# A new order of work around a second attention: who uses bank 0 in which unit, when weighted values run, one reduction for two blocks' maxima, and the split of the maxima on GpSimd

## The reference

```
q, k, v = (einsum('bld,dhe->blhe', x, W) for W in (Wq, Wk, Wv))     # 16 heads of 8
a = einsum('bqhd,bkhd->bhqk', q, k) / 8 ** 0.5
a = softmax(where(tril, a, -inf))
o = einsum('bhqk,bkhd->bqhd', a, v)
return einsum('blhe,hed->bld', o, Wout)
```

## Time and profile before

| what | value |
|---|---|
| median of three runs | 934.86 us |
| the profiled execution | 932.55 us, span 930.8 us |
| PE busy | 842.5 us (91%) |
| DVE busy | 728.3 us (78%) |
| ACT busy | 528.7 us (57%) |
| POOL busy | 465.4 us (50%) |
| mean granted clock of PE | 0.98 |
| the second attention | about 396 to 660 us |
| a middle sequence (1 to 4) of it | 33.24 us |

### The profile page before, as it was taken

How to read it: one execution, slowest core, us unless ns; L and a number is a source line. 1 busy time by engine, 2 the same in 40 slices (tenths; PEclk the granted TensorE clock), 3 DMA queues, 4 the chain that set the end, 5 groups by cost and what they waited for, 6 DMA issues and landing times. The chain is left out here.

```text
span 930.8 us, 17280 instructions
## 1 busy us (share of the span) xinstructions
PE 842.5 (91%) x5977; PEld 556.6 (60%) x5977; DVE 728.3 (78%) x1455; ACT 528.7 (57%) x771; POOL 465.4 (50%) x620
## 2 busy tenths in 40 slices
PE   5899999999778886689999999888889999999997
PEld 4677777775566655334444444443558767776875
DVE  6888998879899995888898998987666656565542
ACT  4677788789566675367777777767423223222311
POOL 4133222224568786236666666456464365345444
PEclk9999999999999999779999999999989999999999
DMA  9300000000000006765545446200000000000000
GB/s 284 93 12 12 11 11 11 0 13 0 16 1 12 1 12 130 142 129 117 111 82 126 106 85 127 52 4 14 12 1 24 1 23 23 23 0 23 11 12 12
DMA packets 36067, 43.79 MB, mean 47 GB/s; under 512 B 4878, under 2 KB 28094, under 8 KB 36000
## 3 DMA queue, kind: packets, MB, share of 16 engines
q1 hardware_dynamic: 36000, 42.93, 19.5%
HBM read 21.81 MB, written 15.09 MB: 40 GB/s over the span
## 5 line engine op out<-in xcount | busy, mean ns | idle before, releaser
L1877 ACT ACTIVATE PT<-PS 128x1024 f32<-128x1024 f32 x160 | 161.5, 1022 | 61.6 <-PE PS L1668 61.3
L1939 POOL TENSOR_SCALAR_AFFINE_SELECT PT<-PT 128x256 f32<-128x256 f32 (+1 forms) x224 | 97.3, 451 | 101.9 <-ACT PT L1877 99.9
L2368 POOL TENSOR_TENSOR PRE_sb<-PRE_sb,VA 128x512 f32<-128x512 f32 x64 | 82.3, 1285 | 125.8 <-DVE PRE_sb L2436 125.7
L2335 ACT ACTIVATE sg_d<-PS 128x512 f32<-128x512 f32 x64 | 38.1, 597 | 154.5 <-PE PS L1397 154.5
L2436 DVE TENSOR_TENSOR PRE_sb<-sg_d,PS 128x512 f32<-128x512 f32 x64 | 44.0, 688 | 79.6 <-ACT sg_d L2335 79.1
L465 ACT ACTIVATE E<-PS,m 128x512 f32<-128x512 f32 x128 | 85.7, 688 | 34.7 <-PE PS L351 25.8
L1979 DVE TENSOR_REDUCE negm<-PS 128x2 f32<-128x1024 f32 x64 | 77.8, 1221 | 20.0 <-PE PS L1657 19.6
L1684 PE MATMUL PS<-PT,VA 128*32 128x512 f32 (+3 forms) x1024 | 89.9, 446 | 3.6 <-POOL PT L1939 3.6
L1650 PE MATMUL PS<-kS,qS 52*128 52x384 bf16 (+3 forms) x512 | 64.3, 311 | 14.7 <-ACT PT L1877 6.9
L514 POOL TENSOR_SCALAR Qs<-Qs 128x1024 f32<-128x1024 f32 x32 | 34.5, 1080 | 81.6 <-ACT Qs L446 81.0
L1668 PE MATMUL PS<-qS,kS 55*128 55x384 bf16 (+3 forms) x512 | 63.4, 307 | 7.5 <-DVE negm L1979 3.5
(11 more groups left out here) (331 smaller groups left out, 2249.5 us busy)
## 6 DMA issues: line engine op xcount, KB each, us to landing
qk_rows<-parts SPq DMA_DIRECT2D x32, 192.0 KB, 2.8
qS<-qk_rows SPq DMA_DIRECT2D x32, 192.0 KB, 4.3
kS<-qk_rows SPq DMA_DIRECT2D x32, 192.0 KB, 4.6
xs_sb<-XN_sb SPq DMA_DIRECT2D x20, 256.0 KB, 2.3
qk_rows<-parts SPq DMA_DIRECT2D x32, 128.0 KB, 2.8
X_sb<-in_x_dram SPq DMA_DIRECT2D x8, 256.0 KB, 6.6
qk_rows<-parts SPq DMA_DIRECT2D x32, 64.0 KB, 2.5
out_dram<-X_sb SPq DMA_DIRECT2D x8, 256.0 KB, 2.3
```

Of the source, the lines that this page charges most:

```text
L1877: nc.scalar.activation(PT[:, quad % 2, u, :], PS[:, b:b + 2, :].rearrange("p b n -> p (b n)"), ACT.Exp).then_inc(exp_ready, 1)
L1939: nc.gpsimd.affine_select(out=v, in_=v, pattern=[[0, 4 if u == 4 else 2], [1, P]], compare_op=ALU.is_ge, fill=0.0, base=0, channel_multipl ...
L2368: nc.gpsimd.tensor_tensor(acts[:, s, f, :], acts[:, s, f, :], W[:, slot, s, :], ALU.mult).then_inc(weighted, 1)
```

## The change

Six things are changed in `attention1`. Bank 0 gets a new table of users: (0,2) OT, (0,4) maxima of half 1, (1,0) V, (1,2) on, (1,4) x, (2,0) q, (2,2) OT, (2,4) maxima of half 0 of the next sequence, (3,2) output, (3,4) k; what waits for what follows it, as do ACT's and DVE's copies. Weighted values of kt 0 run in u = 3; for quads 0 and 1 (and quad 3 of the last sequence) kt 1, 3 and 2 run as one batch in the next quad's u = 1. The two reductions of u = 2, 3 become one per 128 columns, with eight outputs; `negm` has three more slots, and `join_maxima` takes the smallest of the three partial negated maxima of block 2. The split's four instructions run on GpSimd within the periods (on DVE before the first). K's parts are made in (0,1) to (0,4) of the next period and not in quad 3 and (0,1); q's start in (2,1). `factor` moves from (1,0) to (1,1), and the residual `add` from (3,0) to (3,2).

```diff
+M_SLOT = (0, 2, 1, 3)
-        negm = sb("negm", [P, NT, 2, NPAIR])
+        negm = sb("negm", [P, NT + 3, 2, NPAIR])
-        MASK_SLOTS = [(2, 0), (2, 2), (3, 2), (3, 4)]
+        MASK_SLOTS = [(2, 0), (2, 4), (3, 0), (3, 4)]
+        def split_maxima(eng, engine, i, h):
+            ch = Steps(eng, max_steps, i * 2 + h, 4)
+            ch.n = 1
+            hs = slice(4 * h, 4 * h + 4)
+            nm, mr = negm[:, 3:7, :, hs], mrem[:, :, :, hs]
+            mp = lambda k: mpart[:, h, :, :, k, :]
+            ch.wait()
+            ch.link(engine.tensor_copy(mp(0), nm))
+            ch.link(engine.tensor_tensor(mr, nm, mp(0), ALU.subtract))
+            ch.link(engine.tensor_copy(mp(1), mr))
+            engine.tensor_tensor(mp(2), mr, mp(1), ALU.subtract).then_inc(m_parts, 1)
+            ch.end()
...
@@ tensor, weighted_v and period
-                pe.wait_ge(masked, (i * 4 + quad) * 7 + {0: 2, 1: 6, 3: 7}[kts[0]])
+                pe.wait_ge(masked, (i * 4 + quad) * 7 + {(0,): 2, (1,): 6}.get(kts, 7))
-                    if u == 4:
+                    if u == 3:
                         weighted_v(i, slot, quad, (0,))
+                        turn_ot(i - 1, 1)
+                    elif (quad, u) == (0, 4):
+                        if first:
+                            pe.wait_ge(m_row, 1)
+                        else:
+                            pe.wait_ge(o_normed, i * 2)
                         turn_maxima(i, 1)
-                    elif (quad, u) == (0, 3) and not first:
+                    elif (quad, u) == (1, 0) and not first:
                         pe.wait_ge(m_row, i * 2 + 2)
...
+                    elif (quad, u) == (2, 4):
+                        pe.wait_ge(o_normed, i * 2 + 1)
                         turn_maxima(i + 1, 0)
...
-                    elif (quad, u) == (3, 2) and ahead(i):
+                    elif (quad, u) == (3, 4) and ahead(i):
...
-                    if u == 0 or u == 1:
+                    if (quad, u) in ((1, 1), (2, 1)):
+                        weighted_v(i, slot, quad - 1, (1, 3, 2))
+                    elif u == 0 or u == 1:
...
-            weighted_v(LAST, LAST % 2, 3, (1,))
-            weighted_v(LAST, LAST % 2, 3, (3, 2))
+            weighted_v(LAST, LAST % 2, 3, (1, 3, 2))
@@ scalar, period
-                    elif (quad, u) == (0, 2):
+                    elif (quad, u) == (0, 4):
                         keep_maxima(i, 1)
...
@@ gpsimd, period
+                    if (quad, u) == (0, 0) and not first:
+                        split_maxima(pool, nc.gpsimd, i, 1)
+                    elif (quad, u) == (2, 0) and not last:
+                        split_maxima(pool, nc.gpsimd, i + 1, 0)
...
@@ vector, maxima, join_maxima, period
-                    nc.vector.tensor_reduce(negm[:, 2, :, pair], PS[:, b:b + 2, 0:384], AX.X, ALU.max, negate=True)
-                    ins = nc.vector.tensor_reduce(negm[:, 0, :, pair], PS[:, b:b + 2, 384:512], AX.X, ALU.max, negate=True)
+                    ins = nc.vector.tensor_reduce(negm[:, 0:4, :, pair].rearrange("p s r -> p r s"),
+                                                  PS[:, b:b + 2, :].rearrange("p b (s n) -> p b s n", n=P), AX.X, ALU.max, negate=True)
+            def join_maxima(i, h):
                 dve.wait_ge(max_read, i * 20 + 10 * h + 10)
                 hs = slice(4 * h, 4 * h + 4)
+                ins = nc.vector.tensor_reduce(negm[:, 3 + M_SLOT[2], :, hs], negm[:, 0:3, :, hs].rearrange("p s r a -> p r a s"), AX.X, ALU.min)
+                ins.then_inc(max_steps, 1)
...
-                    elif (quad, u) == (3, 0) and not first:
+                    elif (quad, u) == (3, 2) and not first:
                         add(i - 1)
```

More of the change, by code:

```diff
@@ L1731, in period @@
                         maxima(i + 1, 1 - slot, quad, u, ring(n))
-                    if u == 4:
+                    if u == 3:
                         weighted_v(i, slot, quad, (0,))
[L1735 to L1738, removed]
+                    if (quad, u) == (0, 2) and not first:
+                        if i <= LAST - 2:
                             pe.wait_ge(kf_ready, i + 3)
@@ L1778, in period @@
                         ex.turn_selection(pe, 0)
[L1779 to L1782, removed]
                     elif (quad, u) in MASK_SLOTS and last:
                         k = MASK_SLOTS.index((quad, u))
-                        pe.wait_ge(*(((ex.selT_ready, 1), (m_kept, 1), (att_added, i), (m_kept, 3))[k]))
+                        pe.wait_ge(*(((ex.selT_ready, 1), (o_normed, i * 2 + 1), (m_kept, 2), (att_added, i))[k]))
                         ex.mask(0, k).then_inc(m_ready, 1)
@@ L1788, in period @@
                         pr.project(pe, i + 3, 1 - slot, g.wq1, q_ready)
-                    elif (quad, u) == (2, 2) and not last:
+                    elif (quad, u) == (2, 2):
                         if ahead(i):
@@ L1814, in period @@
                         pr.project(pe, i + 3, 1 - slot, g.wk1, k_ready)
-                    if u == 0 or u == 1:
+                    if (quad, u) in ((1, 1), (2, 1)):
+                        weighted_v(i, slot, quad - 1, (1, 3, 2))
+                    elif u == 0 or u == 1:
                         kts = (1,) if u == 0 else (3, 2)
-                        if quad > 0:
-                            weighted_v(i, slot, quad - 1, kts)
-                        elif not first:
+                        if quad == 3:
+                            weighted_v(i, slot, 2, kts)
+                        elif quad == 0 and not first:
                             weighted_v(i - 1, 1 - slot, 3, kts)
@@ L1958, in period @@
                         (ex.low if part else ex.high)(pool, n)
-                    if (quad, u) == (1, 0) and first:
+                    if (quad, u) == (1, 1) and first:
                         factor_and_shift(nc, g, pool, 2 * LAST - 1, 2 * NB, 1, 2)
-                    elif (quad, u) == (1, 0) and i > 1:
+                    elif (quad, u) == (1, 1) and i > 1:
                         factor(i - 2)
                     elif (quad, u) == (0, 1) and behind(i):
+                        pr.first_part_on_pool(pool, i + 2, 1, kf_ready)
+                    elif (quad, u) == (0, 2) and behind(i):
+                        pr.first_rest(pool, i + 2, 1)
+                    elif (quad, u) == (0, 3) and behind(i):
+                        pr.second_part_on_pool(pool, i + 2, 1)
+                    elif (quad, u) == (0, 4) and behind(i):
                         pr.third_part(pool, i + 2, 1)
@@ L2105, in period @@
                         apply(i - 2)
-                    if opens(i, 1) and (quad, u) == (1, 0):
+                    if opens(i, 1) and (quad, u) == (1, 1):
                         ex.keep_x_low(dve, 0, 0)
@@ L2109, in period @@
                         ex.add_logits(dve, 0)
-                    elif opens(i, 1) and (quad, u) == (2, 4):
+                    elif opens(i, 1) and (quad, u) == (3, 0):
                         keep_first_u()
@@ L2123, in period @@
                         mask_first_high(0)
-                    elif last and (quad, u) == (2, 4):
+                    elif last and (quad, u) == (2, 3):
                         mask_first_low(0)
@@ L2133, in _ @@
                 if u == 4 and quad % 2:
-                    split_maxima(0, quad // 2)
+                    join_maxima(0, quad // 2)
+                    split_maxima(dve, nc.vector, 0, quad // 2)
             in_periods(dve, period)
```

113 lines of the change are left out of this document (48 added, 65 removed).

## The result

The changed kernel takes 926.06 us in the median (920.36 to 930.29) against 933.81 (928.85 to 937.58), 18 runs each: ratio 0.9914, 95% interval 0.9895 to 0.9932, 0.9% faster. The forecast was 922.9 (919.0 to 930.5), faster. The profiled execution took 926.10, its span 924.3, for 932.55 and 930.8: 6.5 us less, where the prediction's sum says 12.0.

The account below looks back on a forecast made before the run. PE was taken as the bound, stalling at short steps where maxima wait for the Exp before. Gains of 7.6, 1.2, 1.4, 1.2, 0.2 and 0.4 sum to 12.0 us: 932.55 to 920.55, plus 2.3 gives 922.9 (919.0 to 930.5).

Parts of the forecast that it names:

- Middle sequences: Four equal sequences of the second attention, each 1.9 us shorter (31.3 for 33.2): 7.6 us in all.
- the walk: Step-by-step timing of one sequence on the new table by start-to-start rules; remaining PE waits sum to 1.25 us.
- Sequence 5: Sequence without x, q, k for PE: 30.4 us for 31.6, a gain of 1.2.
- GpSimd's chain: The split's four small instructions on GpSimd, twice per sequence: 1.25 us, hidden with 0.7 to spare before kt 0.
- SP's: Maxima's copy two steps later, so SP issues k's parts and next rows 3 us later; claimed hidden.
- A: Rival: waits only moved; merges and half of DVE's relief leave 3 to 5 us, 931; chance 0.14.
- C: Rival: maxima's DMA as slow in every sequence as in the first, 38 us lost, 961; chance 0.02.
- D: Rival: eight outputs cost more, or PE's order isn't limited as read; within 0.2%, 935; chance 0.06.
- The first sequence: Quads 2 and 3 gain as in the middle, low clock in front: 1.2 us, plus 0.2 for the prologue.
- Sequence 6: Seventh sequence, counted from 0: 31.8 us for 33.2, a gain of 1.4.
- The last: Last sequence, no maxima, ACT leads: moved factor gives back 0.9, merge at the end costs 0.65; net 0.4 gained.
- the merged tail: End of the last sequence: merged kt 1, 3, 2 all wait for the last mask, 0.65 us more.

Follow-up runs that it names:

- the kernel with the selection first: Changed kernel, but in the last sequence's step (1,4) DVE copies the turned selection before the norm's apply; median 920.29 us, ratio 0.9891.
- the DVE half alone: Kernel before, old table, with only the joint reductions, the join and the split on GpSimd; median 934.37 us, ratio 1.0019.
- the kernel with the factor in halves: Changed kernel; last sequence: factor divided over (0,1) and (1,1), apply at (1,2), second expert's first masks earlier, last batch unmerged; 921.78 us, ratio 0.9866.

## Where the prediction was right and where it was wrong

**Middle sequences** (7.6): right, 7.5, with the walk's waits found at their places and sizes. **Sequence 5** (1.2): right, 1.09. Reduction, join, merges, GpSimd's chain, its cover and SP's (no row of PE waits for a transfer): all within 0.1 us, from start to start. Two signs were misjudged. DVE's busy time fell by 1.7 us (30.26 to 28.59) and not by 2.3 to 28.0, and PE's by 0.8 to 30.73 where 31.3 was named. Neither changes the walk, which goes by starts. Rivals A, C and D didn't come. A's claim that "the merges and half of the DVE relief" would be left over is wrong in its second part: in a middle sequence DVE's relief is worth nothing on the old table, and 1.1 to 1.8 us on the new one.

**The first sequence** (1.2, measured -0.49) was given the gain of quads 2 and 3 and none of it was walked. It has no OT, V or output for PE, so with kt gone from u = 4 the steps (1,0) and (1,2) hold little else, and their successors wait for an Exp:

```profile
408.85 0.39 PE L1666 MATMUL PS<-kS,qS 52*128 52x512 bf16 x2 [0.40 <-ACT PT L1894]
...
412.18 0.39 PE L1666 MATMUL PS<-kS,qS 52*128 52x384 bf16 x4 [0.57 <-ACT PT L1894]
```

By the Exp of (2,0) after is 0.86 behind (18.55 for 17.69); from there on it gains 0.37. The clock isn't what sets the two apart: of this sequence, 10.0 us lie in the stretch granted 0.50 in after and 9.7 in before. Where it starts earlier, both tables take less: with 8.0 us of it inside, the kernel with the selection first took 33.60, and with 7.8 us the DVE half alone, on the old table, took 33.24. Compared at like clock the new table costs 0.3 to 0.4 us here, an estimate from these four. The prologue's -0.53 can't be judged: first Exps lie between 393.2 and 399.5 us in the kernels shown here, with different low stretches ahead of them.

**Sequence 6** (31.8 for 33.2, measured 34.38 for 34.96): the earlier trace rows cut it at 627.8, but the scores of (0,0) of sequence 7 start at 629.49, so 33.2 and 32.1 were not lengths of sequences: it lasted 34.96. The new table takes it to 32.97 (in the kernel with the selection first), 2.0 less. After shows 1.4 us more, in one place:

```profile
605.65 2.79 PE L1700 MATMUL PS<-PT,VA 128*32 128x384 f32 x24
```

1.50 elsewhere; the clock granted is 0.50 for 3.4 us there. The walk's 31.8 is 1.2 too low, and was set against a wrong length.

**The last** (0.4 gained, measured -2.07) is the step that failed. The 0.65 of the merged tail is right. The factor, entered as "gives back some 0.9", costs: the prediction saw that it frees quad 0's masks, and didn't put it on the walk of quad 1, nor ask what is queued behind DVE's wait for it. There the selection's copy and the masks of the merged batch both came out, 2.69 us on PE. And the end of the stage was taken as PE's, where it is DVE's.

**The range** held although these misses are of one sign and add up to 5.0 us (1.7, 0.8 and 2.5). It reached 7.6 us above the likeliest, and the chance for "faster" rested on four equal sequences walked step by step, which came as walked. Luck had a part as well: the forecast put the median 2.3 us above the profiled execution, from three runs. Over 18 runs it is 1.3 above it before and level with it after, so the forecast misses by 3.2 us where its sum misses by 5.5.

## What to carry to other kernels

Walk the loop's first and last turns with the same rules as a middle one: work that is hidden in a full turn stands open where its cover is missing, and a piece of 3.6 us on a side engine may need cutting in two. A relief of DVE that was worth nothing in a turn with the old table was worth 1.1 to 1.8 us in most turns with the new one; so test halves together before dropping one, and by turns, since the total of a kernel can hide a gain in the middle behind a loss in the last turn. Where an instruction is shortened to test a cause, read its duration in the new trace first: here it hadn't got shorter. Take boundaries of stretches from a named instruction, never from round times.

## What was not expected of the hardware

- Small casts on GpSimd that wait for nothing follow at 0.16 us each (1.26 for eight of 128x32), those that wait for each other at 0.29; so a chain's price is half its waits.
- A one-input cast on DVE from SBUF to SBUF also stood still while GpSimd worked there, 0.42 for 0.18 us; the prediction had counted instructions with two inputs alone. Beside GpSimd's masks, four one-input instructions on 128x16 took DVE 1.55 us, as long as on 128x128 (1.60). The reverse shows in the last sequence of the kernel with the factor in halves: the chain beside DVE's small two-input work took 0.40, 0.30, 0.35 and 0.42 instead of 0.21, 0.25, 0.21 and 0.25.
- PE's clock was granted at the lower of its levels for 3.4 us in the middle of sequence 6 in four kernels (at 604 to 606 us), and not in three others with the same work there. Those three also lack the low stretch at 256 to 258 us, and their first Exp comes 1.6 to 3.5 us earlier. What decides between the two courses stays open.
